# First-layer expert results scattered to per-token places, and the experts joined in one stage with the attention of batches 2 and 3

## What is computed

```python
xn = layernorm(x);  x = x + attention_0(xn) + experts_0(xn)
xn = layernorm(x);  x = x + attention_1(xn) + experts_1(xn)
```

## Time and profile before

| what | us |
|---|---|
| median of three executions | 1288.99 |
| the profiled execution | 1279.91 |
| its span, first to last instruction | 1278.1 |
| TensorE busy in the span | 1119.2 (88%) |
| VectorE busy | 801.9 (63%) |
| GpSimd busy | 548.8 (43%) |
| ScalarE busy | 524.2 (41%) |

### The profile page before, as it was taken

How to read it: one execution, slowest core, us unless ns; L and a number is a source line. 1 busy time by engine, 2 the same in 40 slices (tenths; PEclk the granted TensorE clock), 3 DMA queues, 4 the chain that set the end, 5 groups by cost and what they waited for, 6 DMA issues and landing times. The chain is left out here.

```text
span 1278.1 us, 20689 instructions
## 1 busy us (share of the span) xinstructions
PE 1119.2 (88%) x5586; PEld 839.3 (66%) x5586; DVE 801.9 (63%) x2224; ACT 524.2 (41%) x1423; POOL 548.8 (43%) x528
## 2 busy tenths in 40 slices
PE   5659999999987999778888999995976997999981
PEld 5436667777776888555555777785544674888861
DVE  5758787666403555379999777625834664666648
ACT  2226766555502444345555555603112331444420
POOL 0656776655200000066565655404276441555540
PEclk9779999999998999989999999998997997999985
DMA  9644442222237666432222222102557932555557
GB/s 330 248 146 164 164 144 86 76 71 72 117 139 187 182 184 182 135 100 71 79 75 71 75 75 76 28 1 78 228 201 212 297 126 61 167 165 166 164 165 246
DMA packets 118684, 177.53 MB, mean 139 GB/s; under 512 B 17231, under 2 KB 86958, under 8 KB 118046
## 3 DMA queue, kind: packets, MB, share of 16 engines
q1 hardware_dynamic: 88910, 123.45, 31.0%
q0 software_dynamic: 13808, 38.19, 8.8%
q10 hardware_dynamic: 15856, 14.56, 3.3%
HBM read 103.95 MB, written 72.19 MB: 138 GB/s over the span
## 5 line engine op out<-in xcount | busy, mean ns | idle before, releaser
L907 POOL TENSOR_TENSOR parts<-wq,parts 128x256 fp32r<-128x256 f32 x64 | 48.8, 762 | 373.9 <-ACT parts L1154 373.9
L1306 PE MATMUL bank<-big_a,probsT 128*128 x760 | 202.1, 361 | 0.3 <-DVE probsT L1386 0.2
L1163 ACT ACTIVATE probs<-bank,negmax 128x256 f32<-128x256 f32 (+3 forms) x256 | 134.7, 536 | 120.1 <-DVE negmax L1078 117.9
L970 PE MATMUL bank<-kT,qT 128*128 128x256 f32 (+3 forms) x512 | 172.1, 458 | 0.0
L986 PE MATMUL bank<-const,probs 128*128 128x128 f32 x640 | 129.6, 276 | 26.2 <-DVE probs L1090 26.1
L1002 PE MATMUL bank<-probsT,big_b 128*128 128x512 f32 (+3 forms) x512 | 149.0, 434 | 0.0
L1306 PEld LDWEIGHTS bank<-big_a,probsT 128*128 128x128 f32 x760 | 131.0, 195 | 21.8 <-issue 2.7
L1078 DVE TENSOR_REDUCE negmax<-bank 128x1 f32<-128x256 f32 (+3 forms) x256 | 113.6, 485 | 47.2 <-PE bank L972 46.1
L1392 DVE TENSOR_TENSOR work<-work,bank 128x96 f32<-128x96 f32 (+1 forms) x190 | 51.4, 270 | 133.0 <-ACT work L1353 131.8
L954 PE MATMUL bank<-parts 128*128 128x512 f32 x256 | 116.9, 492 | 19.9 <-POOL parts L907 15.0
L1275 POOL DMA_INDIRECT yk_dram<-work,place x95 | 91.1, 959 | 90.4 <-DVE place L1415 53.6
(11 more groups left out here) (230 smaller groups left out, 2106.5 us busy)
## 6 DMA issues: line engine op xcount, KB each, us to landing
probs<-xs_dram SPq DMA_DIRECT2D x190, 132.0 KB
work<-khT_dram SPq DMA_DIRECT2D x64, 256.0 KB, 3.3
xs_dram<-big_a SPq DMA_DIRECT2D x16, 792.0 KB, 11.1
ys_dram<-work ACTq DMA_DIRECT2D x95, 128.0 KB, 1.7
wq<-in_wq SPq DMA_DIRECT2D x64, 128.0 KB
yk_dram<-big_a SPq DMA_DIRECT2D x16, 512.0 KB, 4.4
big_a<-yk_dram SPq DMA_DIRECT2D x32, 256.0 KB, 7.0
big_a<-in_gu SPq DMA_DIRECT2D x1, 6144.0 KB, 18.4
```

The lines of the kernel that those rows point to most:

```text
L970: nc.tensor.matmul(s.ps[bank][:, at:at + w], s.qT[:, par, i * P:(i + 1) * P], s.kT[:, par, 0:w], start=True, stop=False)
L1163: nc.scalar.activation(s.probs[:, par, ROW_AT[i]:ROW_AT[i] + (i + 1) * P], s.ps[bank][:, at:at + (i + 1) * P], ACT.Exp, bias=s.negmax[:, p ...
L1306: mm = nc.tensor.matmul(s.ps[2 + i % 2][:, 0:W], rowsT[:, i % 2, k * P:(k + 1) * P], gu[:, k, bass.ds(e * W, W)], start=k == 0, stop=k == ...
```

## The change

**Experts of layer 0** now end as those of layer 1 do. The store to `ys` (L1365) is gone, and so is the table. VectorE does `meet` and `place` for every tile, GpSimd scatters the tile to `yk`, and SP's load of a tile waits for `met` of the tile four before as well. The routing of layer 0 now writes `tile_tag`. `PLACES` goes from 8 to 16, since the result lags by 8 tiles. The small output of `meet` moves out of `wq` into `stats`.

**Combining.** SP loads 128 rows of `yk` at a time, in order, in place of GpSimd's gather. These loads stand in SP's list behind the loads of `wq` and `khb` of the same unit, and each waits for the addition that last used its buffer.

**One stage.** The attention of batches 2 and 3 is part of the block of the experts (`attention0(..., joined)`): each engine's list goes on with it directly. Three waits take the barrier's place: TensorE and the load of `khb` wait until all 95 results are copied, and the first rotation and the first load of results wait until all scatters have landed.

**Zeros.** The 16 stores of zeros to `yk` and the memset for them are gone.

```diff
-PLACES = 8
+PLACES = 16
...
-                link(v.tensor_scalar(s.tile_tag[:], TILE_ROW[:, :], float(1 + EXPERTS), None, ALU.add))
+            link(v.tensor_scalar(s.tile_tag[:], TILE_ROW[:, :], float(1 + EXPERTS * layer), None, ALU.add))
...
 # attention0, SP's list, for each unit u
             if u >= 2:
                 sp.wait_ge(wlow, u - 1)
             sp.dma_start(s.wq[:, par], wq[:, h]).then_inc(w_in[par], 16)
             if u >= 2:
                 sp.wait_ge(k_ready, u - 1)
+            elif joined and u == 0:
+                sp.wait_ge(joined.out_ready, USED_TILES)
             b = rows[bi]
             sp.dma_start(s.khb[:, par], ...)
-            if extra == "scatter" and u < H0:
-                if u == 0:
-                    sp.wait_ge(zero_made, 1)
-                at = u * zeros.shape[1]
-                sp.dma_start(planes[:, at:at + zeros.shape[1]], zeros).then_inc(zeroed, 16)
+            if combining:
+                if u == 0:
+                    for j in range(UNROLL):
+                        sp.wait_ge(joined.y_out[j], joined.landed[j])
+                t = u // 2
+                for k in (2 * (u % 2), 2 * (u % 2) + 1):
+                    if t:
+                        sp.wait_ge(x_added, added_at["row", t - 1, k])
+                    at = TRASH + k * TOKENS + t * P
+                    sp.dma_start(s.gath[0][:, k], d["yk"][at:at + P, :]).then_inc(gathered[k], 16)
...
 # GpSimd's list, for each unit, after qT
-                    if combining:
-                        if t:
-                            pool.wait_ge(x_added, added_at["row", t - 1, k])
-                        nc.gpsimd.indirect_dma_start(
-                            out=s.gath[0][:, k], out_offset=None, in_=d["ys"],
-                            in_offset=bass.IndirectOffsetOnAxis(ap=s.slot_r[:, k, t:t + 1], axis=0),
-                        ).then_inc(gathered[k], 16)
...
 # TensorE's and VectorE's lists, at the start of the attention
+        if joined:
+            pe.wait_ge(joined.out_ready, USED_TILES)
...
         low_of_x(0)
+        if joined:
+            for j in range(UNROLL):
+                dve.wait_ge(joined.y_out[j], joined.landed[j])
         rotate(0)
...
 # expert_block
-    matched = s.wq[:].rearrange("p a k n -> p (a k n)")[:, 0:2 * TOPK]...
+    matched = s.stats[:].rearrange("p t n -> p (t n)")[:, 0:2 * TOPK]...
+        if layer == 0:
+            total = attention0(nc, s, d, lambda name: sem(f"{name}_a2"), [2, 3], "combine", joined)
...
-                    if layer == 1:
-                        sp.wait_ge(met, i - UNROLL + 1)
+                    sp.wait_ge(met, i - UNROLL + 1)
...
-        if layer == 1:
-            @block.gpsimd
+        @block.gpsimd
...
-                if layer == 0:
-                    act.wait_ge(out_ready, i + 1)
-                    act.dma_start(d["ys"][i * P:(i + 1) * P, :], outs[:, j]).then_inc(y_out[j], 16)
...
-                if layer == 1 and i + 2 < N:
+                if i + 2 < N:
                     meet(i + 2)
...
-        attention_block0(nc, s, d, [2, 3], "combine")
```

More of the change, by code:

```diff
@@ L833, with attention0 @@
 LAST_BANKS = (5, 3, 4, 0)
-def attention_block0(nc, s, d, rows, extra):
+def attention0(nc, s, d, sem, rows, extra, joined=None):
     NU = len(rows) * H0
@@ new lines, in gpsimd, with split_low @@
+    def gpsimd(pool):
+        def split_low(u):
+            par = u % 2
+            pool.wait_ge(whigh, u + 1)
+            if u >= 2:
+                pool.wait_ge(q_done, u - 1)
+            nc.gpsimd.tensor_tensor(w_parts[1][:, par], s.wq[:, par], w_parts[0][:, par].bitcast(F32),
+                                    ALU.subtract).then_inc(wlow, 1)
+        split_low(0)
+        split_low(1)
+        for u in range(NU):
+            b, par = rows[u // H0], u % 2
+            pool.wait_ge(kh_in[par], 16 * (u // 2 + 1))
+            if u >= 2:
+                pool.wait_ge(scored, ROWS * (u - 1))
+            nc.gpsimd.tensor_tensor(s.kT[:, par], s.kpT[:, b * SEQ:(b + 1) * SEQ], s.khb[:, par],
+                                    ALU.mult).then_inc(k_ready, 1)
+            if 1 <= u < NU - 1:
+                split_low(u + 1)
+            pool.wait_ge(rope_part, u + 1)
+            nc.gpsimd.tensor_tensor(s.qT[:, par], s.rope_a, s.rope_b, ALU.add).then_inc(q_ready, 1)
+            if not combining:
+                for k in (2 * (u % 2), 2 * (u % 2) + 1):
+                    scatter_tile(nc, s, d, 0, u // 2, gathered, (k,))
+        if not combining:
+            for k in range(TOPK):
+                pool.wait_ge(gathered[k], 16 * TILES)
@@ L893, in _ @@
[L893 to L898, removed]
+            parts.sync(sp)
         @block.gpsimd
         def _(pool):
[L902 to L908, removed]
@@ L1371, in _ @@
                     out(i - LAG)
-            if layer == 0:
-                for j in range(UNROLL):
-                    act.wait_ge(y_out[j], landed[j])
-            else:
-                total.scalar(act)
+            total.scalar(act)
         @block.vector
@@ L1416, in place @@
                                 s.c("trash")[:, i % UNROLL:i % UNROLL + 1], ALU.max).then_inc(placed, 1)
-            if layer == 1:
-                for i in range(2):
-                    meet(i)
+            for i in range(2):
+                meet(i)
             for i in range(2):
                 rowsT_out(i)
-                if layer == 1:
-                    place(i)
+                place(i)
             for i in range(N + 2):
```

592 lines of the change are left out of this document (292 added, 300 removed).

## The result

The changed kernel takes 1294.74 us (median of 14 runs, 1289.86 to 1298.80) against 1285.45 (14 runs) for the kernel before on the same chips: ratio 1.0056, 95% interval 1.0038 to 1.0075. It is slower by 0.6%, where 21.5 us less was forecast, 1.7%.

The account below looks back on a forecast made before the run. VectorE, not TensorE, was taken to bound the first half of the attention of batches 2 and 3. Profiled: 1279.91 - 18.5 - 2.5 - 0.5 = 1258.4 us; 21.5 off the median gives 1267.5, range 1258 to 1287.

Parts of the forecast that it names:

- TensorE covers them all, and I take 0: Experts of layer 0: added additions, scatters and waits stay hidden behind TensorE at 1.46 us a tile; 0 us.
- the far end: Experts of layer 0: if the cover failed, tiles slow to layer 1's 1.62 us; 15 us lost.
- Rival 3: Experts of layer 0 slow to layer 1's pace, by GpSimd or by the loads; 1283 us, chance 0.11.
- The rule of the Trainium skill: Experts of layer 0: GpSimd's DMA descriptors wait while VectorE holds the shared port; estimated 1.63 us a tile, 16 us in all.
- The first half: Attention of batches 2 and 3: loads replacing gathers cut a unit from 8.81 to 7.6 us; 18.5 us with the turn.
- some overlap: First half, batches 2 and 3: `qT` and `kT` end later against the next additions, so 7.21 us is the lower end.
- a ring through the load of `wq`: First half, batches 2 and 3: additions, `wq` load, rotation, `qT`, `kT` set each unit; 5.0 + 2.6, 7.6 us.
- the old overlap: First half, batches 2 and 3: VectorE and GpSimd each stand still while the other has SBUF operands in work.
- rival 4: First half, batches 2 and 3: every `wq` load stands behind a wait for VectorE; 10.3 us a unit, 1307 us, chance 0.09.
- Second half: Second half of the attention of batches 2 and 3: TensorE stays full and VectorE has slack; 0 us.
- Barrier and start: From layer 0's experts to the attention of batches 2 and 3: joining without a barrier wins 2.5 us, ends 0 and 5.
- Zeros: First stage: dropping the 8 MB of zeros relieves the second `wq` load; 0.5 us won, 0 to 2.

Follow-up runs that it names:

- experiment 2: Changed kernel, but GpSimd stores layer 0's results in order with a direct DMA instead of the scatter; 1258.38 us, ratio 0.9793.
- Experiment 10: Changed kernel with layer 1's gate and up products 224 columns wide instead of 256; 1306.14 us, ratio 1.0170.
- 9: Changed kernel, but in layer 0 TensorE turns both halves of each tile's rows and the hidden twice; 1286.19 us, ratio 1.0009.
- 15: Changed kernel with a GpSimd memset of 256 columns, and a wait for its end, behind each scatter of layer 0; 1271.99 us, ratio 0.9927.
- experiment 4: Kernel before, with each unit's two gathers in batches 2 and 3 issued behind `kT` of the next unit instead of behind `qT`; 1264.70 us, ratio 0.9850.
- experiment 8: experiment 4 plus experts and attention of batches 2 and 3 joined in one stage; ScalarE's stores, ordered table and zeros as before; 1265.82 us, ratio 0.9854.
- experiment 1: Changed kernel with the barrier back between layer 0's experts and the attention of batches 2 and 3; 1308.48 us, ratio 1.0182.
- 11: experiment 4 with the first unit's two gathers issued before everything else on GpSimd; 1268.47 us, ratio 0.9853.
- 14: Changed kernel, but each scatter of layer 0 carries 64 rows instead of 128, and the zeros are stored again; 1293.27 us, ratio 1.0142.
- 5: Changed kernel, but layer 0's indirect DMA writes its rows in order instead of to scattered places; 1294.82 us, ratio 1.0075.
- 3: Changed kernel, but layer 0's down product lags by 2 tiles instead of 8; 1294.11 us, ratio 1.0069.
- 12: Changed kernel with eight buffers for results in layer 0 instead of four; 1293.73 us, ratio 1.0077.
- experiment 6: Changed kernel with at most two scatters in flight in layer 0 instead of three; 1307.51 us, ratio 1.0174.
- experiment 13: Changed kernel with a GpSimd memset of 128 columns, and a wait for its end, behind each scatter of layer 0; 1291.81 us, ratio 1.0075.

## Why the prediction was wrong

**What failed: "TensorE covers them all, and I take 0".** The step added up busy times (GpSimd 0.95 of 1.46, VectorE 1.03 of 1.46), and both sums were right: VectorE's additions cost nothing (experiment 2), and GpSimd was busy 61.32 of 120 us. It put at nothing what a scatter does to a third engine. When several indirect DMAs in a row start 1.46 us apart or closer, ScalarE is stopped for 1.5 to 3.3 us every three to seven tiles; each stop lets results pile up, which then are scattered 1.26 us apart, which makes the next one. Cost: +33.4 us, against 0 taken and 15 as the far end. The far end was wrong too: I took layer 1's pace, 1.62, as the worst case, while layer 1 is calm because it is that slow. Experiment 10, which takes work from layer 1, and 9 and 15, which add idle work to layer 0, show both signs. The nearest row was a stage with scatters in it, but at another distance.

**Rival 3** (the experts slow down, 1283) had the right place and half the size. The rule of the Trainium skill weighed there ("SBUF — State Buffer", "SBUF: two separate sides") gave, as an estimate, 16 us through descriptors that wait for VectorE. The trace doesn't agree with it here: a scatter's issue took 0.95 to 0.97 us for all 95 tiles, GpSimd waited only 6.3 us in all for a scatter to land, and what stood still was ScalarE, while VectorE was idle too.

**The first half: right in the mechanism, the size in part by luck.** Forecast 7.6 us a unit and 18.5 in all; measured (707.25 - 598.85) / 14 = 7.74, which is 14.9, the turn to the second half 8.24 from 10.48, which is 2.2, and 2.0 in the first three intervals: 19.1 of the 19.2 in the ledger. The mechanism was tested by itself in experiment 4: `kT` moved away from the additions gives 16.8 without the change. One addition fell from 1061 to 815 ns in this half and a normalisation of 384 columns from 1246 to 482, so some overlap stayed, as forecast:

```profile
L1087 DVE SCALAR_TENSOR_TENSOR x_res<-big_a,weight,x_res 128x256 f32<-128x256 f32 x29 | 23.6, 815 | 1.6
...
L1081 DVE TENSOR_SCALAR probs<-probs,rsum 128x384 f32<-128x384 f32 x15 | 7.2, 482 | 0.0
```

The 7.6 came from a ring through the load of `wq` that was to set every unit. It doesn't: ten of the fourteen units take 6.65 to 7.55 us, near TensorE's own 7.21, and four take 8.1 to 10.0. Three of these four are the ring, closed for one unit, with ScalarE waiting 0.9 to 2.3 us for `wq`. The fourth is the old overlap: VectorE's four normalisations take 3.61 us from 598.45 on, beside GpSimd's `qT` and `kT`. The load of `wq` landed in 2.3 us at the median (2.6 taken) but in up to 4.3; here it is issued behind the additions and two loads of results, and takes 4.2:

```profile
632.87 1.63 DVE L1087 SCALAR_TENSOR_TENSOR x_res<-big_a,weight,x_res 128x256 f32<-128x256 f32 x2
633.94 0.91 SPq L895 DMA_DIRECT2D big_a<-yk_dram  x2
634.90 0.43 SPq L878 DMA_DIRECT2D wq<-in_wq  x1
639.12 0.42 ACT L1147 ACTIVATE parts<-wq 128x256 fp32r<-128x256 f32 x1 [2.25 <-DMA wq<-in_wq]
```

So rival 4's coupling is there, in three units of fourteen; experiment 4, which doesn't have it, takes 7.39 a unit. The mean of the two kinds of units came out near 7.6 without the reason given for it.

**Second half: right** (112.8 us from the nineteenth `qT` to the last, 113.0 before); an addition is longer there now, 879 ns against 480, but TensorE hides it, 106.00 of 106.

**Barrier and start: 2.5 forecast, 0.6 measured.** With stores the join is worth the 2.7 of experiment 8. With scatters, the last copies of ScalarE wait for scatters to land, and the last scatter is issued at 572.36, 3.7 us after the last down product. The last store came 1.0 after it (537.00), so scatters are 2.7 later, where I had allowed 1.5. What I hadn't priced is what the join avoids: a barrier behind scatters costs 11.5 us more than the join (first `qT` at 592.04 in experiment 1, 580.54 after).

**Zeros: 0.5 forecast, not shown.** The 0.7 of the ledger is within the scatter between traces: the last `qT` of batches 0 and 1 starts at 325.59 to 327.84 in the kernels that store the zeros (before, experiments 4, 8, 11 and 14), and at 325.87 to 328.89 in the others.

Sum of the steps other than the one that failed, by the ledger: -20.5 where -21.5 was forecast. Experiment 2 is a kernel with only those: its last `qT` comes 22.3 us earlier than before (793.04), its ratio is 0.979. The step that failed turned it round.

**Open:** why ScalarE of all engines is stopped, and why by an indirect DMA and not by a direct one from the same queue. Excluded are the addresses (5), the number of rows between 64 and 128 (14), the lag (3), waits for landing (12), the joined list (1), VectorE's added work (2) and the layer (9, 10). Not told apart are the indirect DMA as such and the length of its issue, 0.96 us against 0.54 for a store: no run made a direct store as long. The bound lies between 1.46 us (11 gates stopped) and 1.57 (none); at 1.74 and 1.78 there was none either. How many close scatters it takes isn't known: mostly three or four, never a pair in experiment 6, where the next scatter came 1.9 us later or more, but once a pair in experiment 8, where it came after 1.63.

**The better version** is experiment 4: 1264.70 us, 1.5% under the kernel before, with a few lines moved. Experiment 11 hoists one more pair of gathers and isn't told from it.

## What to carry to other kernels

Before you call an added operation hidden because its engine has room, look for its effect on the other engines where it already runs, and ask at which distance it runs there: a calm neighbour with a slower pace is no bound for a faster one. When a forecast comes true, look at the single units behind the mean too: here a mean of 7.74 hid units of 7.2 and of 9. When an engine is long idle with its inputs there, list what every other engine started in that stretch; and test such a coupling by spacing, not only by removing: here an idle instruction was worth 1.3%. And when a change has two parts, test whether the gain can be had alone, here by the order of three instructions.

## What the runs showed of the hardware

- Three or four indirect DMAs in a row that GpSimd issues 1.26 to 1.46 us apart stopped ScalarE for 1.5 to 3.3 us (changed kernel, experiment 13); 1.57 us apart they stopped no gate (15); direct stores by GpSimd, at 1.46 us a tile, didn't either (2).
- The issue of an indirect scatter takes 0.96 us for 128 rows and 0.90 for 64: from 64 rows up their number hardly counts. That of a direct store of 128 rows takes 0.54.
- A barrier of all engines took 10.4 us behind scatters that landed within some 1.6 us, and 2.5 behind stores.
- From its normalisation to its first down product layer 1 took 210 to 211 us in some traces and 213 in others, with the same code there (experiments 3 and 5).
